# A graph layer on one core: where the normalized rows are kept, how the residual is cut, and when keys and gathered edges are fetched

## The chip, the cores and the metric

One core of one Trainium2 chip. The metric is the device time of one execution in microseconds; the kernel before has a median of 561.38 us in 3 runs (560.37 to 562.74). The names of the engines: TensorE is PE, VectorE is DVE, ScalarE is ACT, GpSimd is POOL, SyncE is SP in the profile.

## The reference

The inputs are 6250 rows x of 96 values, 206250 edges sorted by destination, and a row of 96 values for each edge. What is computed:

```python
h = relu((x - mean(x)) / sqrt(var(x) + 1e-5))       # for each of the 6250 rows
m = h[src] + edge_attr                              # one row of 96 for each of 206250 edges
aggr = segment_sum(m, dst, 6250)
out = x + (1 + eps) * h + relu(aggr @ W1 + b1) @ W2 + b2
```

## The kernel before, in words

**Tiles.** The 6250 nodes make 49 tiles of 128 rows, called blocks where they are destinations. Rows are held with the 128 nodes of a tile on the partitions: `x_sb` and `h_sb` are [128, 49, 96] in float32, `hl` holds h as a high and a low half in float16.

**Two ways to sum over edges.** For 45 blocks (NM = 45) `h[src]` is never gathered. VectorE turns the sources and destinations of a block's edges into one-hot matrices (`chunk`, four chunks to a block, L547), TensorE multiplies them to a count matrix in eight steps (`octet`, L961), ScalarE copies each step to `adj` (L810), and in the following block TensorE multiplies `adj` with `hl` in 49 slots (`sum_slots`, L973). The edges' own rows are summed by 80 matmuls with another one-hot matrix (`sum_edges`, L967); they stand behind octet 2 of each block. For the last 4 blocks (GATHERED = 4, numbered j = 0 to 3) GpSimd gathers: 40 indirect DMAs (L477), each adding 128 rows of h from a copy in HBM (`h_rows`) to edge rows that lie in the buffer `gathered[(j + 1) % 2]`. Their sum, again 80 matmuls (L967 on gathered_edges), is attached to one of the 45 blocks: ATTACHED names it. TensorE waits there for `gather_done`, the landing of all 40, in the middle of its queue.

**Order.** All of it is written out by hand: each engine has one queue of instructions, and semaphores with constants join them. There is no planner.

**Before block 0.** SyncE loads the indices and x; VectorE and GpSimd pack the keys and find where each block's edges start (`e_tab`). Then x is normalized. VectorE takes moments (`moments`, L554) of each tile, turns them to variances (`variance`), ScalarE takes the root (`deviation`), VectorE inverts it (`normal`). This is done in two groups, tiles 0 to 23 and 24 to 48. ScalarE then makes h of the first group, tile by tile (L850), VectorE scales the second (L634) and ScalarE applies the relu at once (L854). `high_part` on ScalarE (L841) and `low_part` on VectorE (L577) make `hl`. ScalarE also checks that the edges are sorted (`falls`, L833); TensorE adds that up at the end of block 0 (L1084), and VectorE reads the sum in block 1 (L665).

**Where h lies.** `h_sb` lies in the edge buffers 1 and 2 of three. So the edges of blocks 1 and 2 go to the two gathered buffers instead (`edge_rows`), and the first gathered loads have to wait for block 1's edge sum, SyncE's load of block 4 for both residuals. `residual` (L660) adds (1 + eps) h to x, in two operations of 24 and 25 tiles, at the end of blocks 1 and 2 on VectorE.

**Loads on SyncE.** Each block's load is four pairs of DMAs (L340 destinations, L341 edge rows). Load b is queued once the edge sum of block b - 3 is done. `load_gathered(0)` stands before load 4, `load_gathered(1)` after load 5, the next two behind the gathered sums that free their buffers. A gathered load is four triples (L348 to L350).

**Keys.** Each pair of blocks needs one window of packed keys (L449, an indirect DMA of GpSimd, 3 buffers). Windows 0 to 2 are fetched ahead of the gathers, each later one between gathers: `FETCH_EVERY = 7` with `FETCH_FIRST = 5`, that is before gathers 5, 12, 19 and so on. A fetch waits until TensorE has turned the keys three windows before it (L956). VectorE reads window q in block 2q - 2 (`pick`, L625).

Of the kernel before, what the change touches and what calls it, by code (L numbers as in the profile page):

```python
# [5 lines left out]
F32 = mybir.dt.float32  # L6
# [16 lines left out]
GT = 10  # L23
TURN = 3
# [10 lines left out]
GATHERED = 4  # L35
ATTACHED = (14, 24, 34, 42)
TAIL_CUTS = (8, 18, 34)
FETCH_EVERY = 7
FETCH_FIRST = 5
STORE_LAG = 7  # L40
SQRT_AFTER = 18
KEYS_AFTER = 20


def build(nc, x, src, dst, edge, w1, b1, w2, b2, eps, out):
# [31 lines left out]
    with ExitStack() as ctx:  # L77
# [6 lines left out]
        def sem(name):  # L84
            return ctx.enter_context(nc.semaphore(name))
# [25 lines left out]

        h_sb = edge_home[:, 1:3, :, :, :].rearrange("p k g t c -> p (k g t c)")[:, 0:NT * C].rearrange("p (t c) -> p t c", c=C)
        packed = adj_home[:, :, :, :].rearrange("p k h n -> p (k h n)").bitcast(I32)[:, 0:2 * DW].rearrange("p (e two) -> p e two", two=2)
# [117 lines left out]
        falls_clear = sem("falls_clear")  # L231
        scaled_ready = sem("scaled_ready")

# [60 lines left out]

        ROWS = [slice(0, HALF), slice(HALF, NT)]

        def all_stored(engine):
# [11 lines left out]
        def edge_rows(b):  # L309
            return gathered[b % 2] if b in (1, 2) else edges[b % TURN]  # L310

# [3 lines left out]
        def _(sp):  # L315
# [118 lines left out]
        def _(pool):  # L434
# [87 lines left out]
        def _(v):  # L522
            link = [0]

            def chain(ins):
                link[0] += 1
                ins.then_inc(link_done, 1)
                v.wait_ge(link_done, link[0])
# [23 lines left out]
            def moments(t0, t1):  # L552
                for t in range(t0, t1):
                    last = nc.vector.bn_stats(bn[:, t, :], x_sb[:, t, :])  # L554
                return last

            def variance(k):
                sl = ROWS[k]
                parts = [bn[:, sl, c:c + 1].rearrange("p t o -> p (t o)") for c in range(6)]
# [8 lines left out]
            def normal(k):  # L568
                v.wait_ge(std_ready, k + 1)
                chain(nc.vector.reciprocal(rstd[:, ROWS[k]], rstd[:, ROWS[k]]))  # L570
                nc.vector.scalar_tensor_tensor(shift[:, ROWS[k]], stat[:, 0, ROWS[k]], -0.5, rstd[:, ROWS[k]],
                                               ALU.mult, ALU.mult).then_inc(norm_ready, 1)
# [43 lines left out]
            nc.vector.tensor_copy(span[:, :], oct_ps[0:1, 0, 0:GCOLS])  # L616
            nc.vector.tensor_copy(ends[:, :], oct_ps[0:1, 0, 512:512 + GCOLS])
# [8 lines left out]

            v.wait_ge(x_in[1], 32)
            chain(moments(HALF, NT))
            pick(0)
            variance(1)  # L630
            normal(1)
            v.wait_ge(norm_ready, 2)
            for t in range(HALF, NT):
                last = nc.vector.tensor_scalar(h_sb[:, t, :], x_sb[:, t, :], rstd[:, t:t + 1], shift[:, t:t + 1], ALU.mult, ALU.add)  # L634
            last.then_inc(scaled_ready, 1)

            def passes_needed():

                v.wait_ge(spread_read, 1)
                nc.vector.tensor_scalar(row[:, :], row[:, :], keep[:, 0:1], None, ALU.mult)  # L640
# [15 lines left out]

            def residual(k):
                v.wait_ge(eps_ready, 1)
                v.wait_ge(hl_ready, k + 1)
                nc.vector.scalar_tensor_tensor(x_sb[:, ROWS[k], :], h_sb[:, ROWS[k], :], eps_sb[:, 0:1], x_sb[:, ROWS[k], :],  # L660
                                               ALU.mult, ALU.add).then_inc(res_ready, 1)
# [31 lines left out]
            def finish(b):  # L693
                v.wait_ge(out_done, b + 1)
                if b >= OBS:
                    v.wait_ge(out_stored[b % OBS], 16 * (b // OBS))
                nc.vector.tensor_tensor(ob[b % OBS][:, :], x_sb[:, b, :], mlp_ps[:, OUT_AT:OUT_AT + C], ALU.add).then_inc(out_ready, 1)  # L697
# [15 lines left out]
            for b in range(NM):  # L713
# [82 lines left out]
        def _(act):  # L796
# [33 lines left out]
            nc.scalar.activation(packed[:, :, 1].bitcast(F32), S_lo, ACT.Copy).then_inc(lows_ready, 1)  # L830
            act.wait_ge(falls_clear, 1)
            act.wait_ge(steps_ready, 1)
            nc.scalar.activation(steps.bitcast(F32), steps, ACT.Relu, scale=-1.0, accum_out=falls[:, 0:1]).then_inc(falls_ready, 1)  # L833

            def deviation(k):
                act.wait_ge(var_ready, k + 1)
                nc.scalar.activation(rstd[:, ROWS[k]], stat[:, 2, ROWS[k]], ACT.Sqrt).then_inc(std_ready, 1)

# [4 lines left out]
            deviation(0)  # L843
            act.wait_ge(norm_ready, 1)
            for t in range(HALF):
                if t == KEYS_AFTER:
                    next_keys(0)
                if t == SQRT_AFTER:
                    deviation(1)
                last = nc.scalar.activation(h_sb[:, t, :], x_sb[:, t, :], ACT.Relu, bias=shift[:, t:t + 1], scale=rstd[:, t:t + 1])  # L850
# [85 lines left out]
        def _(pe):  # L936
# [83 lines left out]
            def next_project(n):  # L1020
# [4 lines left out]
                project(hid, OUT_AT).then_inc(out_done, 1)  # L1025

            for b in range(NM):
                here, behind = attached(b), attached(b - 1)
# [126 lines left out]
```

## Time and profile before

| | us |
|---|---|
| median of 3 runs | 561.38 |
| the profiled execution | 559.85 |
| its span | 558.0 |
| TensorE matmul busy | 499.2 (89%) |
| VectorE busy | 504.6 (90%) |
| ScalarE busy | 375.2 (67%) |
| GpSimd busy | 353.9 (63%) |

The span is what the hardware profiler saw from first to last instruction of this one execution; all times in rows count from its start. Busy shares are means over stages with different limits. In a timeline row the first number is the start, the second the time to the end of the last instruction of the row; square brackets hold the idle time before it and what ended it. Successive matmuls overlap, so a row's time can reach past the start of the next.

### The profile page before, as it was taken

To read this page: it belongs to the slowest core of one execution; us is meant where nothing else is said; L and a number is where in the kernel's file an instruction comes from. 1 tells how busy PE (TensorE), PEld (TensorE's weight loads), DVE (VectorE), ACT (ScalarE), POOL (GpSimd) and SP (SyncE) were. 2 spreads that over 40 slices of the span, in tenths; PEclk is the share of its full clock that TensorE was granted. 3 is DMA by queue.
4 is the path that set the end of the run, shared out by engine and by line. 5 is a ranking of instruction groups with operands and counts; after the bars stand their busy time and mean duration, and the time that the engine had idled before them with its cause. 6 is when DMAs were issued, how large, how long until landed. Compare 5 with 4: busy or idle time off the path is not lost.

```text
span 558.0 us, 23440 instructions
## 1 busy us (share of the span) xinstructions
PE 499.2 (89%) x9695; PEld 474.5 (85%) x9695; DVE 504.6 (90%) x676; ACT 375.2 (67%) x613; POOL 353.9 (63%) x200
## 2 busy tenths in 40 slices
PE   0406798999999999999999999999999999999995
PEld 0305788999999999999999999998998999999994
DVE  7989997999999999899998998998998989999840
ACT  0486556677777757776875677677776776775771
POOL 1400048888888888888888887687686478870000
PEclk9999879999999999999999999999999999999998
DMA  6789849999879888999888889988878687985000
GB/s 196 244 283 286 245 122 318 277 307 271 234 196 234 230 210 207 290 262 236 230 232 215 210 217 266 285 215 224 227 206 223 158 241 179 236 226 172 6 11 18
DMA packets 99109, 120.57 MB, mean 216 GB/s; under 512 B 71160, under 2 KB 72792, under 8 KB 98870
## 3 DMA queue, kind: packets, MB, share of 16 engines
q1 hardware_dynamic: 74854, 108.13, 63.3%
q0 software_dynamic: 24144, 10.89, 15.5%
q8 instruction: 78, 1.28, 0.9%
q14 instruction: 33, 0.27, 0.2%
HBM read 112.50 MB, written 6.48 MB: 213 GB/s over the span
## 4 chain that ended last, share of the span: by engine, by line
PE 76%; SPq 7%; ACT 4%; issue 4%; DVE 3%; DMA 3%; POOL 2%; ACTq 0%; DVEq 0%; POOLq 0%
PE agg_ps L973 27%; PE oct_ps L961 21%; PE agg_ps L967 14%; PE key_ps L986 5%; PE mlp_ps L991 4%; SPq L340 3%; ACT adj L810 3%; POOL gathered_edges L477 2%; PE key_ps L978 2%; PE key_ps L979 2%; SPq L339 1%; SPq L341 1%; DMA win<-packed_keys,row_i 1%; ACT hid L826 1%; DVE lo_hot L547 1%
## 5 line engine op out<-in xcount | busy, mean ns | idle before, releaser
L810 ACT ACTIVATE adj<-oct_ps 128x784 f16<-128x784 f32 x360 | 300.6, 867 | 146.9 <-PE oct_ps L961 141.5
L477 POOL DMA_INDIRECT gathered_edges<-h_rows,gather_src x160 | 317.8, 1986 | 97.6 <-DMA gathered_edges<-in_edge_attr 49.1
L973 PE MATMUL agg_ps<-hl,adj 128*128 128x192 f16 x2205 | 227.7, 247 | 0.9 <-issue 0.8
L547 DVE TENSOR_TENSOR lo_hot<-iota_z,key 128x2048 f16<-128x2048 f16 x180 | 219.4, 1219 | 0.0
L961 PE MATMUL oct_ps<-z,lo_hot 128*128 128x98 f16 x2880 | 191.5, 209 | 25.3 <-DVE lo_hot L547 21.0
L547 DVE TENSOR_TENSOR z<-z_marks,key 128x1568 f16<-128x1568 f16 x180 | 174.6, 970 | 22.1 <-PE oct_ps L961 21.7
L961 PEld LDWEIGHTS oct_ps<-z,lo_hot 128*128 128x128 f16 x2880 | 162.5, 99 | 33.5 <-issue 13.9
L973 PEld LDWEIGHTS agg_ps<-hl,adj 128*128 128x128 f16 x2205 | 177.1, 98 | 1.9 <-issue 1.4
L967 PE MATMUL agg_ps<-edges,hot 128*32 128x96 f32 x3440 | 81.1, 250 | 0.0
L967 PEld LDWEIGHTS agg_ps<-edges,hot 128*32 128x32 f32 x3440 | 71.8, 111 | 6.4 <-issue 0.3
L674 DVE TENSOR_TENSOR hot<-iota_w,rel 128x1280 f32<-128x1280 f32 x49 | 73.1, 1492 | 1.7
L449 POOL DMA_INDIRECT win<-packed_keys,row_i x23 | 30.5, 1326 | 33.2 <-PE key_ps L956 24.2
L986 PE MATMUL key_ps<-aggT,w_sb 96*96 96x128 f32 x180 | 30.2, 290 | 2.0 <-issue 1.7
L826 ACT ACTIVATE hid<-key_ps,b_sb 96x128 f32<-96x128 f32 x90 | 27.1, 354 | 2.2 <-PE mlp_ps L991 1.5
L991 PE MATMUL mlp_ps<-w_sb,hid 97*128 97x96 f32 (+1 forms) x180 | 26.6, 270 | 0.7 <-ACT hid L826 0.7
L986 PEld LDWEIGHTS key_ps<-aggT,w_sb 96*96 96x96 f32 x180 | 20.9, 162 | 7.4 <-issue 1.3
L991 PEld LDWEIGHTS mlp_ps<-w_sb,hid 97*128 97x128 f32 (+1 forms) x180 | 23.6, 191 | 1.7 <-ACT hid L826 0.9
L697 DVE TENSOR_TENSOR ob<-x_sb,mlp_ps 128x96 f32<-128x96 f32 x45 | 11.2, 249 | 15.4 <-PE mlp_ps L991 15.4
L978 PE MATMUL key_ps<-ident,agg 128*96 128x128 f32 x90 | 18.2, 285 | 0.4 <-ACT agg L816 0.4
L979 PE MATMUL key_ps<-ident,agg 128*96 128x128 f32 x90 | 17.4, 276 | 0.0
L816 ACT ACTIVATE agg<-agg_ps 128x192 f32<-128x192 f32 x45 | 14.9, 330 | 3.7 <-PE agg_ps L973 3.2
L798 ACT ACTIVATE key<-key_ps 128x512 f16<-128x512 f32 x23 | 13.8, 600 | 0.4 <-PE key_ps L979 0.4
(126 smaller groups left out, 204.2 us busy)
## 6 DMA issues: line engine op xcount, KB each, us to landing
edges<-in_edge_attr SPq DMA_DIRECT2D x172, 480.0 KB
gathered_edges<-in_edge_attr SPq DMA_DIRECT2D x24, 480.0 KB
dst<-in_dst SPq DMA_DIRECT2D x180, 5.0 KB
gathered_edges<-h_rows,gather_src POOLq DMA_INDIRECT x160
out<-ob SPq DMA_DIRECT2D x45, 48.0 KB
packed_keys<-adj SPq DMA_DIRECT2D x1, 1632.0 KB, 6.3
h_rows<-edges SPq DMA_DIRECT2D x1, 1200.0 KB, 9.2
h_rows<-edges SPq DMA_DIRECT2D x1, 1152.0 KB, 9.2
```

What stands on the lines that cost most here:

```text
L449: nc.gpsimd.indirect_dma_start(out=to[:, :, :].rearrange("p e two -> p (e two)"), out_offset=None, in_=keys_dram, in_offset=bass.IndirectO ...
L477: nc.gpsimd.indirect_dma_start(out=gathered[k][:, g, t, :], out_offset=None, in_=h_dram, in_offset=bass.IndirectOffsetOnAxis(ap=gather_src ...
L547: return nc.vector.tensor_tensor(out.rearrange("p t (w two) -> p t w two", two=2), marks[0:out.shape[0], 0:width].rearrange("p (o w two) - ...
L674: return nc.vector.tensor_tensor(hot[buf][:, :, :], iota_w[:, :].rearrange("p (o w) -> p o w", o=1).broadcast_to([P, GROUPS * GT, GROUP]), ...
L810: return nc.scalar.activation(adj[k][:, :, 2 * OCT * o:2 * OCT * (o + 1)].rearrange("p h (t q) -> p t h q", q=2), oct_ps[:, o % 2, :].rear ...
L826: last = nc.scalar.activation(to[0:C, j, :], key_ps[0:C, at + P * j:at + P * (j + 1)], ACT.Relu, bias=b1_sb[:, j:j + 1])
L961: last = nc.tensor.matmul(oct_ps[:, o % 2, P * t:P * t + ZW], lo_hot[o // 2][:, at, :], z[o // 2][:, at, :], start=True, stop=True)
L967: last = nc.tensor.matmul(sums[GROUP * g:GROUP * (g + 1), :], hots[:, g * GT + t, :], rows[:, g, t, :], start=fresh and t == 0, stop=False ...
L973: last = nc.tensor.matmul(agg_ps[buf][:, 0:2 * C], adj[buf][:, h, :], hl[:, h, :], start=False, stop=(h == NT - 1), skip_group_check=True)
L978: nc.tensor.matmul(key_ps[0:C, TURN_AT:TURN_AT + P], agg[:, 0:C], ident[:, :], start=True, stop=False)
L986: last = nc.tensor.matmul(key_ps[0:C, at + P * j:at + P * (j + 1)], w1_sb[:, j, :], turned_sums[:, :], start=True, stop=True)
L991: last = nc.tensor.matmul(mlp_ps[:, at:at + C], hidden_values[0:C + 1 - j, j, :], w2_sb[0:C + 1 - j, j, :], start=(j == 0), stop=(j == H - 1))
```

## The change

- `h_sb` now lies in the two gathered buffers (tiles 0 to 39 in buffer 0, tiles 40 to 48 in buffer 1). All blocks load their edges into the edge buffers proper, and the third load no longer waits for the order check's input.
- The residual is cut into nine pieces, `RES`: tiles 40 to 48 first, then eight pieces of 5 tiles. They stand at the end of blocks 2 to 10. `finish(b)` waits for the piece that holds its tile.
- The first gathered load (buffer 1) stands behind load 5 and waits for the first piece; the second (buffer 0) stands behind load 14 and waits for all nine.
- ATTACHED goes from (14, 24, 34, 42) to (14, 22, 32, 42).
- The statistics are made in three groups: tiles 0 to 15, 16 to 31, 32 to 48. ScalarE makes h of all 49 tiles, and the order check comes behind the first root.
- The fourth window is fetched at once; later ones at 3 for each 25 gathers, before gathers 0, 9, 17, 25, 34 and so on.

```diff
-ATTACHED = (14, 24, 34, 42)
+ATTACHED = (14, 22, 32, 42)
-FETCH_EVERY = 7
-FETCH_FIRST = 5
+FETCH_EVERY = 25
+FETCH_PER = 3
-SQRT_AFTER = 18
-KEYS_AFTER = 20
+KEYS_AFTER = 24
+RES_FIRST = 40
+RES_ROWS = 5
...
-        h_sb = edge_home[:, 1:3, :, :, :].rearrange(...)
+        h_sb = gather_home[:, :, :, :, :].rearrange(...)
...
+        THIRDS = [slice(0, 16), slice(16, 32), slice(32, NT)]
+        RES = [(RES_FIRST, NT)] + [(t, t + RES_ROWS) for t in range(0, RES_FIRST, RES_ROWS)]
...
-            return gathered[b % 2] if b in (1, 2) else edges[b % TURN]
+            return edges[b % TURN]
... (SyncE)
-            sp.wait_ge(steps_ready, 1)
             load(2)
...
                 sp.wait_ge(edges_done, b - TURN + 1)
-                if b == TURN + 1:
-                    load_gathered(0)
-                    sp.wait_ge(res_ready, 2)
-                    sp.wait_ge(h_stored, 32)
                 load(b)
                 if b == TURN + 2:
+                    sp.wait_ge(h_stored, 32)
+                    sp.wait_ge(res_ready, 1)
+                    load_gathered(0)
+                if b == TURN + 2 + len(RES):
+                    sp.wait_ge(res_ready, len(RES))
                     load_gathered(1)
... (GpSimd)
-            fetched = WINS
+            fetched = WINS + 1
+            fetch(WINS)
             pool.wait_ge(h_stored, 32)
...
-                        if (j * GROUPS + g) * GT + t >= (fetched - WINS) * FETCH_EVERY + FETCH_FIRST and fetched < MPAIRS:
+                        if ((j * GROUPS + g) * GT + t) * FETCH_PER >= (fetched - WINS - 1) * FETCH_EVERY and fetched < MPAIRS:
... (VectorE, before block 0)
-            moments(0, HALF // 2)
+            chain(moments(0, 16))
+            variance(0)
...
+            normal(0)
...
-            chain(moments(HALF // 2, HALF))
-            variance(0)
+            moments(16, HALF)
+            v.wait_ge(x_in[1], 32)
+            moments(HALF, 26)
...
-            normal(0)
+            chain(moments(26, 32))
+            variance(1)
...
-            v.wait_ge(x_in[1], 32)
-            chain(moments(HALF, NT))
             pick(0)
-            variance(1)
             normal(1)
-            v.wait_ge(norm_ready, 2)
-            for t in range(HALF, NT):
-                last = nc.vector.tensor_scalar(h_sb[:, t, :], x_sb[:, t, :], rstd[:, t:t + 1], shift[:, t:t + 1], ALU.mult, ALU.add)
-            last.then_inc(scaled_ready, 1)
+            nc.vector.tensor_copy(span[:, :], oct_ps[0:1, 0, 0:GCOLS])
+            nc.vector.tensor_copy(ends[:, :], oct_ps[0:1, 0, 512:512 + GCOLS]).then_inc(spread_read, 1)
+            chain(moments(32, NT))
+            variance(2)
+            normal(2)
... (VectorE, blocks)
-                if b in (1, 2):
-                    residual(b - 1)
+                if 2 <= b < 2 + len(RES):
+                    residual(b - 2)
... (ScalarE)
+            deviation(0)
             act.wait_ge(falls_clear, 1)
             act.wait_ge(steps_ready, 1)
             nc.scalar.activation(steps.bitcast(F32), steps, ACT.Relu, scale=-1.0, accum_out=falls[:, 0:1]).then_inc(falls_ready, 1)
...
+            for t in range(NT):
+                for k in range(1, 3):
+                    if t == THIRDS[k].start:
+                        deviation(k)
+                for k in range(3):
+                    if t == THIRDS[k].start:
+                        act.wait_ge(norm_ready, k + 1)
+                last = nc.scalar.activation(h_sb[:, t, :], x_sb[:, t, :], ACT.Relu, bias=shift[:, t:t + 1], scale=rstd[:, t:t + 1])
+                if t + 1 == HALF:
+                    last.then_inc(h_ready, 1)
+                if t + 1 == KEYS_AFTER:
+                    next_keys(0)
+                if t + 1 == HALF:
+                    high_part(0)
             last.then_inc(h_ready, 1)
-            high_part(0)
-            act.wait_ge(scaled_ready, 1)
-            nc.scalar.activation(h_sb[:, ROWS[1], :], h_sb[:, ROWS[1], :], ACT.Relu).then_inc(h_ready, 1)
             high_part(1)
```

## Rows read from the trace of the kernel before

**Rows 1.** Page, busy time, share of the span, instructions

```profile
PE 499.2 (89%) x9695; PEld 474.5 (85%) x9695; DVE 504.6 (90%) x676; ACT 375.2 (67%) x613; POOL 353.9 (63%) x200
```

**Rows 2.** Windows: busy us of each engine, granted clock, DMA share, 100 to 500 us

```profile
100.00:500.00 400.00, 395.24 (x7856) 378.66 (x7849) 378.56 (x437) 288.16 (x473) 325.56 (x172) 1.00 0.88 232
```

**Rows 3.** Timeline of TensorE, edge sums: blocks 2, 5, 14, 14 gathered, 22, 34 gathered

```profile
75.92 2.16 PE L967 MATMUL agg_ps<-gathered_edges,hot 128*32 128x96 f32 x80
...
109.77 1.86 PE L967 MATMUL agg_ps<-edges,hot 128*32 128x96 f32 x80
...
204.57 1.86 PE L967 MATMUL agg_ps<-edges,hot 128*32 128x96 f32 x80
206.24 1.83 PE L967 MATMUL agg_ps<-gathered_edges,hot 128*32 128x96 f32 x80
...
292.17 1.86 PE L967 MATMUL agg_ps<-edges,hot 128*32 128x96 f32 x80
...
424.84 1.83 PE L967 MATMUL agg_ps<-gathered_edges,hot 128*32 128x96 f32 x80
```

**Rows 4.** Windows, GpSimd's busy time alone: two rows of L477, then L449

```profile
77.30:177.50 100.20, 78.75 (x40) 1.00 0.92 251
177.50:280.40 102.90, 81.37 (x40) 1.00 0.90 238
...
177.50:280.40 102.90, 7.56 (x6) 1.00 0.90 238
```

**Rows 5.** Waits of the whole kernel: us in total, times, longest

```profile
POOL win L449 <- PE key_ps L956: 24.2, 6, 8.5
```

**Rows 6.** Timeline of GpSimd, first and third gather

```profile
77.37 3.62 POOL L477 DMA_INDIRECT gathered_edges<-h_rows,gather_src  x1 [49.13 <-DMA gathered_edges<-in_edge_attr]
...
83.75 1.68 POOL L477 DMA_INDIRECT gathered_edges<-h_rows,gather_src  x1 [0.30 <-issue]
```

**Rows 7.** Timeline of ScalarE before block 0

```profile
26.29 6.55 ACT L850 ACTIVATE edges<-x_sb,shift,rstd 128x96 f32<-128x96 f32 x18 [1.51 <-DVE shift L571]
...
35.61 2.12 ACT L841 ACTIVATE hl<-edges 128x2304 f16<-128x2304 f32 x1
...
44.35 1.57 ACT L810 ACTIVATE adj<-oct_ps 128x784 f16<-128x784 f32 x2 [0.24 <-PE oct_ps L961]
```

**Rows 8.** Timeline of VectorE, blocks 0 to 4

```profile
39.55 0.20 DVE L668 TENSOR_TENSOR rel<-dst,gbase 128x40 f32<-128x40 int32 x1
...
55.60 0.15 DVE L665 TENSOR_SCALAR keep<-mlp_ps 128x1 f32<-128x1 f32 x1
...
64.30 2.61 DVE L660 SCALAR_TENSOR_TENSOR x_sb<-edges,eps_sb,x_sb 128x2304 f32<-128x2304 f32 x1
66.83 0.19 DVE L668 TENSOR_TENSOR rel<-dst,gbase 128x40 f32<-128x40 int32 x1
...
76.74 2.71 DVE L660 SCALAR_TENSOR_TENSOR x_sb<-edges,eps_sb,x_sb 128x2400 f32<-128x2400 f32 x1
...
95.86 0.29 DVE L625 TENSOR_SCALAR keyT<-win,base 128x128 f32<-128x128 int32 x1 [2.69 <-DMA win<-packed_keys,row_i]
```

**Rows 9.** Timeline of TensorE, end of block 0

```profile
53.08 0.34 PE L1084 MATMUL mlp_ps<-falls,ones 127*128 127x1 f32 x2
```

**Rows 10.** Tile view of the key windows, all 23

```profile
DMA to landing us min/median/max: 4.2/4.9/6.2
```

**Rows 11.** Timeline of SyncE's queue: first gathered load, loads of blocks 4 and 5

```profile
63.81 0.33 SPq L348 DMA_DIRECT2D gather_src<-in_src  x1
...
80.20 0.33 SPq L340 DMA_DIRECT2D dst<-in_dst  x1
...
86.68 0.33 SPq L340 DMA_DIRECT2D dst<-in_dst  x1
```

**Rows 12.** Windows, columns as in rows 2, TensorE in block 2

```profile
70.60:76.00 5.40, 5.38 (x46) 5.00 (x50) 5.40 (x7) 2.57 (x3) 0.00 (x0) 0.50 0.71 193
```

More of the change, by code:

```diff
@@ L110, in build @@
         keyT = [sb(f"keyT{k}", [P, P]) for k in range(2)]
-        h_sb = edge_home[:, 1:3, :, :, :].rearrange("p k g t c -> p (k g t c)")[:, 0:NT * C].rearrange("p (t c) -> p t c", c=C)
+        h_sb = gather_home[:, :, :, :, :].rearrange("p k g t c -> p (k g t c)")[:, 0:NT * C].rearrange("p (t c) -> p t c", c=C)
         packed = adj_home[:, :, :, :].rearrange("p k h n -> p (k h n)").bitcast(I32)[:, 0:2 * DW].rearrange("p (e two) -> p e two", two=2)
@@ L231, in build @@
         falls_clear = sem("falls_clear")
-        scaled_ready = sem("scaled_ready")
         win_in = [sem(f"win_in{k}") for k in range(WINS)]
@@ L557, in variance @@
             def variance(k):
-                sl = ROWS[k]
+                sl = THIRDS[k]
                 parts = [bn[:, sl, c:c + 1].rearrange("p t o -> p (t o)") for c in range(6)]
@@ L569, in normal @@
                 v.wait_ge(std_ready, k + 1)
-                chain(nc.vector.reciprocal(rstd[:, ROWS[k]], rstd[:, ROWS[k]]))
-                nc.vector.scalar_tensor_tensor(shift[:, ROWS[k]], stat[:, 0, ROWS[k]], -0.5, rstd[:, ROWS[k]],
+                chain(nc.vector.reciprocal(rstd[:, THIRDS[k]], rstd[:, THIRDS[k]]))
+                nc.vector.scalar_tensor_tensor(shift[:, THIRDS[k]], stat[:, 0, THIRDS[k]], -0.5, rstd[:, THIRDS[k]],
                                                ALU.mult, ALU.mult).then_inc(norm_ready, 1)
@@ L615, in _ @@
             nc.vector.tensor_scalar(e_tab[:, :], e_raw[:, :], float(ELAST), None, ALU.min).then_inc(tab_ready, 1)
-            nc.vector.tensor_copy(span[:, :], oct_ps[0:1, 0, 0:GCOLS])
-            nc.vector.tensor_copy(ends[:, :], oct_ps[0:1, 0, 512:512 + GCOLS])
             nc.vector.tensor_copy(reach_row[:, :], key_ps[0:1, 2 * P:3 * P]).then_inc(spread_read, 1)
-            normal(0)
+            chain(moments(26, 32))
+            variance(1)
             def pick(q):
@@ L625, in pick @@
                 nc.vector.tensor_scalar(keyT[q % 2][:, :], win[q % WINS][:, :, 0], base[:, q:q + 1], 1.0 / SPREAD, ALU.subtract, ALU.mult).then_inc(keys_ready, 1)
-            v.wait_ge(x_in[1], 32)
-            chain(moments(HALF, NT))
             pick(0)
-            variance(1)
             normal(1)
-            v.wait_ge(norm_ready, 2)
-            for t in range(HALF, NT):
-                last = nc.vector.tensor_scalar(h_sb[:, t, :], x_sb[:, t, :], rstd[:, t:t + 1], shift[:, t:t + 1], ALU.mult, ALU.add)
-            last.then_inc(scaled_ready, 1)
+            nc.vector.tensor_copy(span[:, :], oct_ps[0:1, 0, 0:GCOLS])
[3 more added lines that the diff above has]
+            normal(2)
             def passes_needed():
-                v.wait_ge(spread_read, 1)
+                v.wait_ge(spread_read, 2)
                 nc.vector.tensor_scalar(row[:, :], row[:, :], keep[:, 0:1], None, ALU.mult)
@@ L655, in passes_needed, with residual @@
                 nc.vector.tensor_scalar(need_i[:, 3:4], need[:, 0:1], float(MAXR), None, ALU.min).then_inc(need_ready, 1)
[L657 to L660, printed above, removed]
+            def residual(piece):
+                rows = slice(*RES[piece])
+                if piece == 0:
+                    v.wait_ge(eps_ready, 1)
+                    v.wait_ge(hl_ready, 2)
+                nc.vector.scalar_tensor_tensor(x_sb[:, rows, :], h_sb[:, rows, :], eps_sb[:, 0:1], x_sb[:, rows, :],
                                                ALU.mult, ALU.add).then_inc(res_ready, 1)
@@ L694, in finish @@
                 v.wait_ge(out_done, b + 1)
+                if b < RES_FIRST:
+                    v.wait_ge(res_ready, 2 + b // RES_ROWS)
                 if b >= OBS:
@@ L830, in _ @@
             nc.scalar.activation(packed[:, :, 1].bitcast(F32), S_lo, ACT.Copy).then_inc(lows_ready, 1)
-            act.wait_ge(falls_clear, 1)
-            act.wait_ge(steps_ready, 1)
-            nc.scalar.activation(steps.bitcast(F32), steps, ACT.Relu, scale=-1.0, accum_out=falls[:, 0:1]).then_inc(falls_ready, 1)
             def deviation(k):
                 act.wait_ge(var_ready, k + 1)
-                nc.scalar.activation(rstd[:, ROWS[k]], stat[:, 2, ROWS[k]], ACT.Sqrt).then_inc(std_ready, 1)
+                nc.scalar.activation(rstd[:, THIRDS[k]], stat[:, 2, THIRDS[k]], ACT.Sqrt).then_inc(std_ready, 1)
             def high_part(k):
@@ L843, in _ @@
             deviation(0)
-            act.wait_ge(norm_ready, 1)
-            for t in range(HALF):
-                if t == KEYS_AFTER:
+            act.wait_ge(falls_clear, 1)
+            act.wait_ge(steps_ready, 1)
+            nc.scalar.activation(steps.bitcast(F32), steps, ACT.Relu, scale=-1.0, accum_out=falls[:, 0:1]).then_inc(falls_ready, 1)
+            for t in range(NT):
[9 more added lines that the diff above has]
+                if t + 1 == KEYS_AFTER:
                     next_keys(0)
-                if t == SQRT_AFTER:
-                    deviation(1)
-                last = nc.scalar.activation(h_sb[:, t, :], x_sb[:, t, :], ACT.Relu, bias=shift[:, t:t + 1], scale=rstd[:, t:t + 1])
+                if t + 1 == HALF:
+                    high_part(0)
             last.then_inc(h_ready, 1)
-            high_part(0)
-            act.wait_ge(scaled_ready, 1)
-            nc.scalar.activation(h_sb[:, ROWS[1], :], h_sb[:, ROWS[1], :], ACT.Relu).then_inc(h_ready, 1)
             high_part(1)
@@ L1025, in next_project @@
                 project(hid, OUT_AT).then_inc(out_done, 1)
+            pe.wait_ge(spread_read, 2)
             for b in range(NM):
```

## The prediction

> **What bounds the kernel now.** I read the page's busy lines first: TensorE is busy 89% of the span and GpSimd only 63% [rows 1], so GpSimd looks idle enough to be ignored. It can't be, as the next views show. Between 100 and 500 us TensorE is busy 395.24 of 400 us at full clock [rows 2]: in the steady part it is the bound and has nothing to catch up with, so whatever stops it there is lost. TensorE's timeline gives the places: the first gathered sum starts at 206.24 (block 14), block 22's own edge sum at 292.17, the third gathered sum at 424.84 (block 34) [rows 3]. The row of block 22 matters most: a gathered sum attached to block 22 would start 1.67 us after that edge sum (206.24 less 204.57), at 293.84. The windows over GpSimd's gathers show that the first 40 gathers take 100.2 us and the second 40 take 102.9 us [rows 4]. Of the 102.9, the busy time is 81.37 + 7.56, the rest is 0.30 between instructions, so GpSimd works through without a pause; it waits only 24.2 us in all, before window fetches [rows 5], and those are late ones (its longest is 8.5 us). The four times 40 gathers are one serial chain of some 400 us, which starts with the first gather at 77.37 [rows 6]. The second 40 end at 280.4 and are used in block 24, two pitches after block 22, near 315: 35 us of slack. That slack is what the change spends.
>
> **Part 1, three groups, ScalarE makes all of h.** VectorE loses 25 scalings at the start; ScalarE does 49 tiles instead of 24, at 6.55 / 18 = 0.36 us each [rows 7]. VectorE must still finish the third group's statistics before block 0, and their root stands behind ScalarE's tile 31. ScalarE: check of the order done near 22.9, 16 tiles to 28.8, then a wait for the second group until about 30.4 (its factors stand behind the first key window on VectorE), 8 tiles to 33.3, key copy 0.6, high part 2.12 [rows 7] to 36.0, 8 tiles to 38.9, root, and VectorE's last factors at 39.6. Block 0 started at 39.55 [rows 8]. So nothing is gained there: estimate 0, between -1 and +1.
> ScalarE then makes 17 more tiles (6.2) and the second high part (2.2) and comes to block 0's sums at 48.1 instead of 44.35 [rows 7]. That is 3.8 us late. VectorE hides most of it, since it has buffers for a block ahead, until it reads the order check's result in block 1: that product ran at 53.08, behind block 0's last octet, and moves to about 57.6, while VectorE would read it at 55.60 [rows 8, 9]. Cost up to 2.3 us, with 0 as the other end.
>
> **Part 2, the residual.** Blocks 1 and 2 lose operations of 2.61 and 2.71 us, about 5.2 together (64.30 to 66.83 is 2.53) [rows 8]. These stood on VectorE, which has no idle time until 95.86. The nine pieces: 2.53 us for 2304 elements is about 1.04 ns each plus some 0.1; 480 elements take 0.6, the first of 864 takes 1.0. Blocks 2 and 3 get 1.6 back; blocks 4 to 10 have seven of 0.6, against TensorE's pitch: nine blocks from 109.77 to 204.57 [rows 3], 10.53 each. VectorE is busy 378.56 of 400 us [rows 2], 10.0 of each 10.53, so with a piece its block takes 10.6: cost 0 to 0.7.
>
> **Part 3, the fetches.** The fourth window is fetched at once. In block 4 VectorE waited 2.69 us for it, from 93.2 to 95.86 [rows 8]; this goes. Later windows come every 8.33 gathers, about 20.9 us for two blocks of 21, and each window is asked for more than a block before it is needed: the fifth, sent with the first gather near 97, lands after 4.2 to 6.2 us [rows 10], and block 6 wants it near 113. No cost.
>
> The start therefore gains, by block 5: 5.2 - 1.6 + 2.7 - 2.3 = 4.0, less about 0.5 for what TensorE still needs by itself: 3.5. After the pieces 2.9 is left. If the gathers were in time, that would be the result.
>
> **Part 4, where the gathers start.** The buffers now hold h, so the first gathered loads are queued one block later and behind one more load. Before, they were issued from 63.81, and the first gather came at 77.37, 13.56 later [rows 6, 11]. Now SyncE first waits for block 2's edge sum, which ended at 75.92 + 2.16 = 78.08 [rows 3]. In the changed kernel VectorE starts block 2 between 2.5 us earlier and 0.2 earlier (2.53 gained, 2.3 lost): I take 76.6. Then 0.7 to the first issue, 6.48 for a block's load (80.20 to 86.68) [rows 11], and 12 to 13.56 for the gathered loads and their landing. First gather: 76.6 + 0.7 + 6.5 + 12.8 = 96.6, range 93.5 to 99. That is 19 us later than 77.37.
>
> **Part 5, the chain to block 22.** With 8.33 gathers per fetch each of the first two blocks has 5 fetches. The first: 100.2 as before. The second: 102.9 less one fetch of 1.5 (7.56 / 6, and 0.3 between) is 101.4 [rows 4]. Three corrections. The first gather took 3.62 where the following ones take 1.7 [rows 6]: it lay beside the large residual operation, which now is elsewhere (-1.7). The small pieces lie beside gathers: 0 to 0.6 each for six of them; I take +1.5. When TensorE stops, VectorE soon stops too and the gathers run faster: the shortest takes 1.54 + 0.30 against 2.33 on average, for some 6 us: -1.2. Sum: 201.6 - 1.4 = 200.2, between 197 and 205. Landing of the last gather after GpSimd's issue is not shown; windows land 4.2 to 6.2 after their start [rows 10], so 3.0 to 5.0 after the issue of 1.2; I take 3.5. Ready: 96.6 + 200.2 + 3.5 = 300.3.
> The first of these three corrections is where a rule and a row differ. The first gather (77.37 to 80.99) ends exactly 1.54 after the residual operation's end at 79.45, as though it had been held back all the while [rows 6, 8]. The Trainium skill (SBUF — State Buffer, Who interferes with whom) says that a VectorE instruction with two SBUF inputs holds up only GpSimd's reads, and infers that it does not hold up descriptor generation. By that rule the pieces would cost the gathers nothing and the chain would be 1.5 us shorter; the single row speaks against it.
>
> **Part 6, what it costs.** Block 22 wants the rows at 293.84 - 2.9 = 290.9. TensorE stands for 9.4 us. Against the kernel before, where it would go on at 293.84 with nothing to wait for, the net shift is 300.3 - 293.8 = +6.5: the gain at the start cancels out of this, since TensorE waits for GpSimd whatever it arrives at. And the clock: after VectorE kept TensorE idle before 70.6 its granted clock was 0.50 of full (1.2 GHz) from 70.6 to 76.0, 5.38 us busy [rows 12]; the same work at 2.4 GHz is 2.7 us. I add 2.7, between 0 and 3.5.
> The Trainium skill (TensorE: Matmul & The Clock Gate, What's actually happening) has the same two levels and says that an idle TensorE falls to the lower; it agrees with this row.
> After block 22 nothing stalls again. Gathers three end near 297 + 100 + 3.5 = 400.5, and block 32 comes at about 300.3 + 2.7 + 109 = 412 (20 blocks with two attached ones took 218.6, from 206.24 to 424.84 [rows 3]); gathers four near 499, block 42 near 521. At block 14: ready at 96.6 + 98.5 to 101.7 + 3.5, at most 201.8, wanted at 203.3. A late arrival there would only use up time that block 22 loses anyway. The second gathered load is issued after block 11's edge sum and lands near 193, before the 195 at which it is wanted; the margin is thin.
> Sum: 6.5 + 2.7 = +9.2. The profiled execution took 559.85 for a span of 558.0; it lies 1.5 below the median of 561.38, so the forecast is span 567.2, median 561.38 + 9.2 = 570.6.
>
> **The rivals.**
> 1. The gathers are in time and the start's gain stays. For it: page and waits call GpSimd idle a third of the time. Against it: that idle time is the 49.1 us before the first gather and the end. It needs readiness by 290.9, 9.4 us earlier, so first gather by 87.2 or 2.1 us per gather for 2.33. Time: 561.4 - 2.9 = 558.5; faster. Chance 0.08.
> 2. The stall exists but is small: first gather at 93.5, chain 197, landing 3.0, no clock loss: ready at 293.5, shift -0.3 to about +2.5. Time 561 to 564, no change. Chance 0.08.
> 3. The stall is larger, or a second one comes: the second gathered load is late (SyncE reaches it behind stores), or windows come too late because their fetches now ride on gathers that start 19 us later. Each gather block's wait adds 3 to 8 us: 574 to 579, slower. For it: the load's thin margin. Against it: the windows' lead of more than a block. Chance 0.14.
> 4. ScalarE's late start delays block 0 further and half clock holds TensorE through blocks 1 to 3: 2 to 3 us, but every microsecond passes one for one to the first gather. Time 572 to 574, slower; it is inside the main case's range. Chance 0.10.
> The forecast itself has 0.60. Half a per cent, 2.8 us, is about what a measurement can tell from no change: faster 0.08, same 0.08, slower 0.84. The range takes the main case from 565 to 575 and reaches into rivals 2 and 3: 563.5 to 577.
>
> **What would show it.** The first gather of the changed kernel between 93.5 and 99. A wait of TensorE of about 9 us in block 22, ahead of the gathered edge sum, ended by a gather's landing, and the only long one; clock at 0.5 behind it. No VectorE wait in block 4, edge sum of block 5 about 3.5 earlier than at 109.77. GpSimd without waits for keys. Wrong it would be if gathers went at clearly under 2.3 us each, or if the first began before 90; then rival 1 decides.

## The result, and the profile after

The changed kernel takes 565.30 us (median of 10 runs, 562.94 to 567.96), the one before 559.13 in ten runs beside it (557.05 to 562.74; the 561.38 of the forecast was the median of the first three of them). The ratio is 1.010, with 95% between 1.0072 and 1.0129: slower by 6.2 us. Runs more than 1.5% above the fastest of the same kernel are left out of every ratio here, so a ratio need not be the quotient of the two medians. Forecast was slower by 9.2, to 570.6. The mechanism was right; the size forecast was half as large again as the one measured.

The profiled execution took 564.01 us for a span of 562.1, so the two traces lie only 4.1 us apart. The busy line of its page, and a row of its waits (us in total, times, longest):

```profile
PE 499.5 (89%) x9695; PEld 473.1 (84%) x9695; DVE 500.5 (89%) x666; ACT 382.0 (68%) x638; POOL 347.3 (62%) x200
```

```profile
PE agg_ps L977 <- issue: 6.3, 3, 5.4
```

Busy times are what they were [rows 1]; nothing in the totals shows a loss. GpSimd's wait before its chain has grown from 49.1 us [rows 6] to 62.3, its waits for keys [rows 5] are gone but for half a microsecond, and TensorE has two new waits, both ahead of gathered sums. TensorE's timeline shows where (L977 is the old L967): blocks 2, 14, 14 gathered, 22, 22 gathered.

```profile
70.79 1.86 PE L977 MATMUL agg_ps<-edges,hot 128*32 128x96 f32 x80
...
199.03 1.86 PE L977 MATMUL agg_ps<-edges,hot 128*32 128x96 f32 x80
201.93 1.86 PE L977 MATMUL agg_ps<-gathered_edges,hot 128*32 128x96 f32 x80 [1.04 <-DMA gathered_edges<-h_rows,gather_src]
...
290.57 1.86 PE L977 MATMUL agg_ps<-edges,hot 128*32 128x96 f32 x80
297.86 3.72 PE L977 MATMUL agg_ps<-gathered_edges,hot 128*32 128x96 f32 x80 [5.43 <-issue]
```

Read against [rows 3]: block 2 is 5.1 us early, block 14 still 5.5, block 22 only 1.6, since block 14 lost 1.0 to the gathers and 2.25 in a gap behind. The gap belongs to this execution: in a second trace of the same kernel (experiment 2) it is missing, block 22 comes 2.2 us sooner, and the wait there is 8.10 us. Block 22's gathered sum could have started at 292.24 and starts at 297.86. "issue" in the bracket means that this view finds no releaser. I take it to be the landing of the gathers, which TensorE's program waits for at this place; GpSimd's timeline holds the first and the last of them:

```profile
92.67 3.25 POOL L451 DMA_INDIRECT win<-packed_keys,row_i  x1 [62.31 <-DMA gathered_edges<-in_edge_attr]
96.22 2.61 POOL L480 DMA_INDIRECT gathered_edges<-h_rows,gather_src  x1 [0.30 <-issue]
...
292.61 2.22 POOL L480 DMA_INDIRECT gathered_edges<-h_rows,gather_src  x1 [0.30 <-issue]
```

The second 40 gathers are issued by 294.83, and TensorE goes on 3.03 us after. TensorE's granted clock behind that wait is 0.50, in a window of 5.2 us:

```profile
297.80:303.00 5.20, 5.14 (x87) 4.78 (x88) 0.00 (x0) 0.00 (x0) 4.29 (x4) 0.50 1.03 279
```

GpSimd's gathers (busy time alone), the first and the second 40:

```profile
92.60:197.10 104.50, 82.30 (x40) 1.00 0.89 236
197.30:294.90 97.60, 76.58 (x40) 1.00 0.91 241
```

### The profile page after: what moved, and what is told of

Its sections match the earlier page's. It is cut to its first block, busy times and chain, and to the rows that moved or that the text cites. A ratio compares the mean times of both kernels' runs of the same rounds, so it can differ in the third digit from the quotient of the medians.

```text
span 562.1 us, 23456 instructions
## 1 busy us (share of the span) xinstructions
PE 499.5 (89%) x9695; PEld 473.1 (84%) x9695; DVE 500.5 (89%) x666; ACT 382.0 (68%) x638; POOL 347.3 (62%) x200
## 4 chain that ended last, share of the span: by engine, by line
PE 57%; POOL 16%; SPq 8%; issue 7%; ACT 4%; DVE 4%; DMA 3%; ACTq 0%; DVEq 0%; POOLq 0%
PE agg_ps L983 20%; PE oct_ps L971 15%; POOL gathered_edges L480 14%; PE agg_ps L977 12%; PE key_ps L996 4%; SPq L342 3%; PE mlp_ps L1001 3%; ACT adj L817 2%; SPq L341 2%; POOL win L451 2%; SPq L343 2%; PE key_ps L988 1%; PE key_ps L989 1%; DMA gathered_edges<-h_rows,gather_src 1%; DVE lo_hot L550 1%
## 5 line engine op out<-in xcount | busy, mean ns | idle before, releaser
L480 POOL DMA_INDIRECT gathered_edges<-h_rows,gather_src x160 | 310.0, 1937 | 48.8 <-issue 48.8
L971 PEld LDWEIGHTS oct_ps<-z,lo_hot 128*128 128x128 f16 x2880 | 160.8, 99 | 32.4 <-issue 18.3
L977 PE MATMUL agg_ps<-edges,hot 128*32 128x96 f32 x3600 | 85.5, 249 | 0.9 <-issue 0.9
L977 PEld LDWEIGHTS agg_ps<-edges,hot 128*32 128x32 f32 x3600 | 75.3, 111 | 7.1 <-issue 0.7
L451 POOL DMA_INDIRECT win<-packed_keys,row_i x23 | 31.7, 1377 | 74.0 <-DMA gathered_edges<-in_edge_attr 62.3
L857 ACT ACTIVATE gathered_edges<-x_sb,shift,rstd 128x96 f32<-128x96 f32 x49 | 17.9, 453 | 1.1 <-DVE shift L574 1.1
```

The source lines that it names most:

```text
L451: nc.gpsimd.indirect_dma_start(out=to[:, :, :].rearrange("p e two -> p (e two)"), out_offset=None, in_=keys_dram, in_offset=bass.IndirectO ...
L480: nc.gpsimd.indirect_dma_start(out=gathered[k][:, g, t, :], out_offset=None, in_=h_dram, in_offset=bass.IndirectOffsetOnAxis(ap=gather_src ...
L971: last = nc.tensor.matmul(oct_ps[:, o % 2, P * t:P * t + ZW], lo_hot[o // 2][:, at, :], z[o // 2][:, at, :], start=True, stop=True)
L977: last = nc.tensor.matmul(sums[GROUP * g:GROUP * (g + 1), :], hots[:, g * GT + t, :], rows[:, g, t, :], start=fresh and t == 0, stop=False ...
```

## The experiments

All runs but four (named below) were made on chips where the kernel before takes 559 to 561 us. Each ratio is against the kernel before on the same chip.

**1. The attachment list alone.** Three kernels; first the changed one with the old list:

```diff
-ATTACHED = (14, 22, 32, 42)
+ATTACHED = (14, 24, 34, 42)
```

> The changed kernel with the old attachment list (14, 24, 34, 42). Theory (the gathers start 15 us later and TensorE waits for them in blocks 14 and 22): the wait in block 22 and the half clock behind it go; the gathered sum of block 14 still starts about 1 us late. The trace of the changed kernel was 1.6 us ahead of the one before at block 22's own edge sum, so this ends 1 to 2 us under the kernel before, about 557.5. Rival A (the nine residual pieces, the three groups or the new pace of the fetches cost the time themselves, all along): the list changes nothing, 564 to 566.

Measured: 556.41 us, ratio 0.9927 (0.9898 to 0.9956). The loss is gone and a gain is there; only block 14 still waits (1.7 us in this trace). Next, a first block two later:

```diff
-ATTACHED = (14, 22, 32, 42)
+ATTACHED = (16, 24, 34, 42)
```

> The changed kernel with the attachment list (16, 24, 34, 42). Theory: no gathered sum is waited for any more; the lead of 5.5 us that the changed kernel had at block 13 is kept to the end: 559.1 - 5.5 = 553.6, between 553 and 555.5. Rival A: 564 to 566. Rival B (only block 22 matters, block 14's loss was a stall of instruction supply that has nothing to do with the gathers): as the list (14, 24, 34, 42), about 557.5.

Measured: 554.24 us, ratio 0.9893 (0.9858 to 0.9927), and twice more, once on another chip, 555.19 (0.9912, 0.9878 to 0.9947) and 555.27 (0.9916, 0.9894 to 0.9939). The expectations of those two:

> The changed kernel with the list (16, 24, 34, 42), again. Theory: 1% faster than the kernel before on either kind of chip, since nothing in it waits for a gather; 10 to 11 us under the changed kernel where there are no gaps in the supply, 0 to 4 where there are.

> Nine pieces with the list (16, 24, 34, 42), the third time. Expected 0.9 to 1.1% under the kernel before, as twice before.

This kernel beats both: the one before by 4 to 7 us in its three runs, the changed one by 10.5 on the chip that ran both. All of the change is in it but the list. How much of that is block 14's is less clear. Theory had 2 to 4 us for it, and the three medians lie 1.1 to 2.2 us under the 556.41 of the list (14, 24, 34, 42); rival B (nothing) is unlikely but not excluded. And the new list in the kernel before:

```diff
-ATTACHED = (14, 24, 34, 42)
+ATTACHED = (14, 22, 32, 42)
```

> The kernel before with the new attachment list (14, 22, 32, 42) alone. Theory: the second 40 gathers are done at 280.4 plus a landing of 3, and block 22 wants them at 293.8, so nothing waits: the kernel before within 1 us. Rival C (attaching to block 22 and 32 costs by itself, by the order of the work around it): 4 to 6 us over the kernel before.

Measured: 559.08 us, ratio 0.9975 (0.9947 to 1.0003). Its trace has no wait at block 22. So the list costs nothing by itself, the rest of the change costs nothing by itself, and the two together lose 1%. Rival A (pieces, groups and fetches cost the time themselves) and rival C (the early attachment costs by itself) are out.

**2. The start of the chain, moved both ways.** The first gathered load ahead of load 5:

```diff
-                load(b)
                 if b == TURN + 2:
                     sp.wait_ge(h_stored, 32)
                     sp.wait_ge(res_ready, 1)
                     load_gathered(0)
+                load(b)
```

> The changed kernel with the first gathered load queued ahead of load 5, not behind it. Theory: the whole chain of gathers starts 6.5 to 7 us earlier (first window fetch near 86 for 92.7), the second 40 are ready near 291.2 for 297.9; block 14 no longer waits; block 22 waits about 3 us, perhaps without the half clock. Time: 291.2 - 293.8 = -2.6 against the kernel before, plus 0 to 2.7 for the clock: 556.5 to 559.5. Rival A: no change against the changed kernel, 564 to 566.

Measured: 561.05 us, ratio 0.9957 (0.992 to 0.9994); its single runs spread from 554.4 to 565.3. The median is level with the 560.77 of the kernel before on this chip, 4 us under the changed kernel, and over the 556.5 to 559.5 expected. The gathered sum of block 22 starts at 293.86, 4.0 us earlier than in the changed kernel. The mechanism held, the distance did not: the chain starts at 89.5 instead of 86, since the load now waits for the first residual piece (the piece ends at 75.43, the load is issued at 76.57). Then one block later (`TURN + 3` for `TURN + 2`):

> The changed kernel with the first gathered load one block later, again, now beside the changed kernel on one chip. Theory: ready 10 us later, so 9 to 11 us over the changed kernel where its blocks wait for gathers; on a chip with gaps the part that the slower TensorE leaves, 3 to 8. Rival A: within 2 us.

and the changed kernel again, beside it on one chip:

> The changed kernel itself, beside the ones below on one chip, since the last call ran on a chip where TensorE stood for instructions in many small gaps (0.2 to 0.4 us each) and everything took 14 to 18 us longer. Where TensorE is slower and the gathers keep their pace, the gathers come in time: on such a chip theory expects the changed kernel 0 to 1% faster than the one before; on one without the gaps 0.7 to 1.3% slower, as first measured. Rival A (the cost is in pieces and fetches): slower by the same share on both.

Measured: the later one 568.88 us (1.0144, 1.0082 to 1.0206), the changed one 565.67 (1.0088, 1.0053 to 1.0123). Slower by 3.2, where 9 to 11 was expected: a miss. The later kernel's single runs spread from 563.6 to 574.9, so the 3.2 is known to a few us only, but not as 9. TensorE's timeline of the later one in block 22, then GpSimd's windows:

```profile
294.94 1.86 PE L977 MATMUL agg_ps<-edges,hot 128*32 128x96 f32 x80
301.90 2.41 PE L977 MATMUL agg_ps<-gathered_edges,hot 128*32 128x96 f32 x55 [5.11 <-issue]
```

```profile
104.10:201.80 97.70, 75.81 (x40) 1.00 0.93 244
201.80:299.20 97.40, 76.27 (x41) 0.98 0.87 230
```

The chain starts 10.4 us after the changed kernel's that was run beside it (93.8) and its rows are taken 3.5 us later (301.90 for 298.36): the first 40 took 97.7 instead of 103.9 (93.8 to 197.7). One gather more falls into the second window's edges. The difference in time, 3.2, fits the 3.5 by which the rows are late. What does not hold is that the chain keeps its length. The 6.2 us are found in single gathers: in the changed kernel's trace three of the first 40 take 3.9 us, some 2 us over the others, and in the later kernel's none does. Experiment 3 takes these up.

**3. What sets the length.** Two residual pieces, neither beside a gather:

```diff
-RES_ROWS = 5
+RES_ROWS = 40
```

> The changed kernel with two residual pieces, again, beside the changed kernel. On the chip with gaps its first 40 gathers with 5 fetches took 100.6 us against 104.4 in the changed kernel's trace. Theory P: the second 40 are ready 3 to 4 us earlier than in the changed kernel, and where block 22 waits for them the time is 2 to 4 us less although VectorE spends 3.6 us more in block 3. Theory Q: the two are equal within 1.5 us.

Measured, beside the changed kernel: 563.93 us (1.0054, 1.0018 to 1.0089) for 565.67. Rows of TensorE and GpSimd's windows:

```profile
290.11 1.86 PE L977 MATMUL agg_ps<-edges,hot 128*32 128x96 f32 x80
294.55 2.02 PE L977 MATMUL agg_ps<-gathered_edges,hot 128*32 128x96 f32 x80 [2.58 <-issue]
```

```profile
93.10:191.90 98.80, 77.19 (x40) 0.99 0.91 246
191.90:288.80 96.90, 75.64 (x41) 1.00 0.91 236
```

98.8 for 103.9: in these two traces the rows are ready 3.8 us earlier. The medians differ by 1.7, between the 2 to 4 of theory P and the 1.5 of theory Q, with VectorE having 3.5 more to do in block 3. The trace of the two pieces is that of the fastest of its twelve runs (558.50), so it shows more than the median does. Whether the pieces are what costs the gathers 5 us, the next kernel asked. In the changed kernel three gathers take 3.9 us (at 113.83, 135.04 and 156.27), each across a piece with the comparison behind it. The first of them, and VectorE's comparison:

```profile
113.83 3.90 POOL L480 DMA_INDIRECT gathered_edges<-h_rows,gather_src  x1 [0.30 <-issue]
```

```profile
117.08 1.49 DVE L679 TENSOR_TENSOR hot<-iota_w,rel 128x1280 f32<-128x1280 f32 x1
```

The kernel with the pieces in the middle of their blocks:

```diff
-                for c in range(2, CHUNKS):
-                    chunk(b, c)
                 if 2 <= b < 2 + len(RES):
                     residual(b - 2)
+                for c in range(2, CHUNKS):
+                    chunk(b, c)
```

> The changed kernel (list 14, 22, 32, 42) with each residual piece between chunks 1 and 2 of its block instead of behind chunk 3, where relative and comparison follow. Theory P2 (a gather is held while float32 operations of VectorE with two SBUF inputs follow each other for over 2 us: piece, relative, comparison): no gather of 3.9 us is left in blocks 5 to 10, the first 40 gathers with 5 fetches take 98 to 100.5 us for 104, the second 40 are ready 4 to 6 us earlier; the time is 3 to 6 us under the changed kernel (0.9 to 1.0% over the kernel before), so within 0.5% of the kernel before. Theory Q (the long gathers come from elsewhere, as the queue of transfers): chain 104, time 0.9 to 1.0% over the kernel before.

Measured: 563.05 us, ratio 1.0066 (1.0048 to 1.0084). In between: the chain's first part is 101.8, the rows are taken at 294.16, and two long gathers are there after all, the first of them here:

```profile
103.20 4.65 POOL L480 DMA_INDIRECT gathered_edges<-h_rows,gather_src  x1 [0.30 <-issue]
```

No piece runs between 102.3 and 112.2 in that kernel, only the comparison at 106.46. Theory P2 as I stated it falls. The traces go further: a piece is neither needed nor enough for a long gather. Not needed, since the kernel before with the new list (experiment 1), whose residual is long done by then, has four of them in its first 40, here the first and the comparison that it runs across:

```profile
120.05 4.02 POOL L477 DMA_INDIRECT gathered_edges<-h_rows,gather_src  x1 [0.30 <-issue]
```

```profile
122.68 1.49 DVE L674 TENSOR_TENSOR hot<-iota_w,rel 128x1280 f32<-128x1280 f32 x1
```

Its first 40 take 108.6 us (75.35 to 183.96), where the kernel before, which is the same program up to block 22, took 100. Not enough, since in experiment 2 the later start has six pieces beside its first 40 gathers, not one gather over 2.9 us, and 97.7 us. In all 17 traces 44 gathers take 3.8 us or more; a piece lies beside 27 of them and none beside 17. All 44 start 2.6 to 3.3 us before a comparison and run into it, but many that start there are not long. On the usual chips the first 40 take 98 to 100 us in the traces with none or one of them, 102 with two, 102 to 105 with three. So 98.8 against 103.9 is one long gather against three. With nine pieces at the end of their blocks, nine of ten traces have three or four in the first 40, with two pieces it is one or two in four traces; the pieces may well favour them, but that they cause them is not shown. What makes a gather long stays open.

**4. Nine pieces or two, with nothing waiting for gathers** (list 16, 24, 34, 42):

> Two pieces with the list (16, 24, 34, 42), beside the next run on one chip. VectorE spends 4.2 us in block 3 for 0.6, nine pieces give 1.3 back by block 13. Expected 2 to 3 us over the next run. Rival: equal.

Measured: 559.25 us (0.9972, 0.9947 to 0.9997) beside 555.27 for nine pieces. 4.0 us, over the 2 to 3 expected: nine pieces over nine blocks are the better form, 0.71 us each where VectorE had 0.5 idle, against one of 4.21 in block 3.

**5. Four runs on a slower chip.** There the kernel before took 578.96 us:

> The changed kernel with the first gathered load one block later (behind load 6). Theory (the time is set by when the second 40 gathers are ready, one for one): the chain starts about 10.5 us later, block 14 waits about 10 us more than in the changed kernel, block 22 is reached later by that and the second 40 are ready near 308; the time is 10 to 11 us over the changed kernel, about 575. Rival A (slack is left in the chain, the cost is elsewhere): within 2 us of the changed kernel, 564 to 567.

> The changed kernel with the residual in two pieces, tiles 40 to 48 at the end of block 2 and tiles 0 to 39 at the end of block 3, so that none lies beside a gather; the second gathered load then stands behind load 7. Theory P (a residual piece holds GpSimd's gathers up for as long as it runs): the first 40 gathers with their 5 fetches take about 100 us for 104.4, the second 40 are ready near 293.4 for 297.9. Theory Q (VectorE's operations with two inputs do not hold up the making of descriptors): 104.4 as before. VectorE is the bound in block 3, so 3.6 us of the lead go there; time with P 559 to 562, with Q 563.5 to 566.

> As the run with two pieces, with the attachment list (16, 24, 34, 42), so that no gathered sum is waited for. It measures what nine pieces over nine blocks are worth by themselves against 4.2 us of VectorE in block 3: lead at block 5 about 3.2 for 6.8 us, of which the nine pieces give 1.3 back up to block 13. Expected 2 to 2.5 us over the kernel with nine pieces and this list: 556 to 557. Rival: pieces are hidden in either place: 554 to 554.5.

> The changed kernel with the list (16, 24, 34, 42) and without the early fetch of the fourth window: it is fetched with the first gather. Block 4 wants it at 88.6 and it would land at 92.7 + 5 = 97.7; VectorE waits 9 us there, TensorE 7. Expected 7 us over the kernel with this list, 561 to 562: then the early fetch does not gain the 2.7 us that VectorE waited before, it avoids a wait of 9 which the later start of the gathers would have made. Rival: the wait is hidden by buffers, 556 to 557.

The last one:

```diff
-            fetched = WINS + 1
-            fetch(WINS)
+            fetched = WINS
```

Neither the changed kernel nor the one with nine pieces and the list from 16 was run on this chip, and the kernel before has no trace there, so of the expectations only those on the traces can be held against the runs directly. Measured: one block later 576.18 (0.9963, 0.993 to 0.9996), two pieces 574.47 (0.9937, 0.9905 to 0.9968), two pieces with the list from 16 574.26 (0.9932, 0.9904 to 0.9961), no early fetch 583.86 (1.009, 1.0057 to 1.0124). The first is a miss: about 575 was expected for a usual chip, 10 us over the changed kernel and so 16 over the kernel before; here it is not slower than the kernel before. The waits are there: its trace (of its slowest execution, 585.64) has 5.56 us in block 14 and 5.38 in block 22, which TensorE reaches at 303.7. Why it is no slower than the kernel before all the same is not shown. Its first 40 gathers take 104.1 us with three long ones, against the 97.7 and none of the same kernel in experiment 2. The two pieces have no wait in block 22, and their first 40 take 100.6 us, near the 100 of theory P, with two long ones among them; as nothing waits, the list from 16 changes nothing either (574.26 for 574.47). The fetch is clear in its size if not to the microsecond, 9.6 us over the kernel next to it, which has two pieces for nine, with VectorE's wait in block 4:

```profile
99.39 0.29 DVE L629 TENSOR_SCALAR keyT<-win,base 128x128 f32<-128x128 int32 x1 [9.38 <-DMA win<-packed_keys,row_i]
```

9.38 us, where 9 were expected. The early fetch is not a gain of the 2.69 us of [rows 8] put on top; it pays for the later start of GpSimd's chain. In the same trace GpSimd waits 5.55 us before gather 41 for the second gathered load: the wait that rival 3 feared.

## Why the prediction was right in kind and too large

**Right.** The slack of 35 us in the second 40 gathers was spent by a start 15.3 us later (77.37 to 92.67) and an attachment two blocks, some 21 us, earlier. The long wait stands in block 22 (5.4 and 8.1 us in two traces of the changed kernel, about 9 forecast), it goes away with the old list, the clock behind it is 0.50, and the start's gain cancels: readiness decides. In six traces on the usual chips that wait there, span less the start of block 22's gathered sum is 264.2, 266.7, 264.2, 264.8, 262.0 and 266.1; in the kernel before, 558.0 - 293.84 = 264.2, where 2.5 us of gaps happen to stand for the 2.7 us of the clock. The clock term was sized right: from that sum (297.86) to block 23's edge sum at 311.16 pass 13.30 us, behind block 14 of the kernel before 10.58 (206.24 to 216.82); 2.7 forecast, 2.7 found. VectorE's wait in block 4 is gone.

**The terms that were off.** Ready at 300.3 was forecast, 297.86 came.

- Part 4, the start: "I take 76.6" for block 2's edge sum; it ended at 70.79 + 1.86 = 72.65. This is the step that failed. It has three parts. Block 0 starts on VectorE at 37.66, not 39.6 (part 1 had said that nothing is gained there, within 1 us): the second group's factors did not wait for the key window until 30.4 but were there at 28.8, as the window was there at 27.86. The order check cost VectorE 1.13 us, not 2.3. And I took the distance of 11.25 us from VectorE's block start to the edge sum's end over from a trace in which TensorE stood at half clock there [rows 12]; here TensorE is at full clock from 66 to 73 and the distance is 9.03 (63.62 to 72.65). The first gathered load was issued at 80.67, 3.1 us before the 83.8 of the forecast, and 12.0 us passed from there to the start of the chain instead of 12.8: -3.9 together. The sign named for this, the first gather between 93.5 and 99, came true at 96.22 by luck: a window fetch stands ahead of that gather, and the chain, whose start is what the sum puts at 96.6, began at 92.67. For the same reasons block 5's edge sum came 6.8 us early for 3.5 forecast, which changes nothing behind block 22.
- Part 5, the length: 200.2 forecast, 202.2 found (92.67 to 294.83). The sum hid two larger errors: the first part took 104.4 instead of 100.0 (three gathers of 3.9), the second 97.8 instead of 100.2. That the first part can be 97.7, 98.8 or 108.6 by the number of its long gathers is something that the sum had no term for, and that the two errors partly cancel is luck. I had the pieces at +1.5. By the inference in the Trainium skill (SBUF — State Buffer, Who interferes with whom) they would cost nothing; experiment 3 leaves open whether they do. The single row that I set against it, the first gather's end 1.54 us behind the residual's, is no special case: nearly all gathers end so behind a change of instruction on VectorE (last section).
- Landing: 3.5 forecast, 3.03 found.
- Block 14 was forecast with 1.5 us to spare and came 1.0 late; as forecast, this has no price of its own, since block 22 waits anyway.

Readiness by itself makes 4.0 of the 6.5 forecast, with the clock 6.7, against 6.2 measured in ten runs. The two traces show 4.1, because TensorE in the kernel before has gaps of 0.57, 0.82 and 1.11 us in blocks 22, 30 and 34 that the other trace has not.

**The base.** 561.38 was 2.2 us high; a forecast of a difference should have been read so.

**A sentence that was wrong although the result did not show it.** Rival 4 said that every microsecond passes one for one to the first gather, and its time took it from there to the end. In the one pair of traces that tries it, 10.4 us at the start of the chain became 3.5 at its end; the rest went into long gathers that one has and the other has not. And rival 1 needs 2.2 us per gather, not 2.1: its 9.4 us are 0.12 for each of 80.

## What to carry to other kernels

An engine that the profile's page calls 62% busy can be the one that sets the time, if its work is one chain with a fixed first and last point: compute the chain's end and the consumer's arrival, and treat their difference as a budget that every edit of start and consumer draws on. Two edits that are harmless alone can overdraw it together. When a constant is tuned (here the list), retune it after the edits that move its inputs: (16, 24, 34, 42) turned a loss of 1% into a gain of 1%. And leave room in the budget: the length of the same 40 gathers differed by 6 to 9 us between two traces of the same instructions (97.7 and 104.1, 100 and 108.6).

## What the runs showed of the hardware that was not expected

**Chips differ by 18 us in the same program.** On the slower one, TensorE has many gaps with no releaser inside a row of 80 matmuls. The same kernel (two pieces) on it, TensorE's timeline in a block, and its window beside that of the usual chip:

```profile
242.53 1.14 PE L977 MATMUL agg_ps<-edges,hot 128*32 128x96 f32 x29
244.03 1.35 PE L977 MATMUL agg_ps<-edges,hot 128*32 128x96 f32 x51 [0.36 <-issue]
```

```profile
100.00:500.00 400.00, 389.03 (x7541) 367.41 (x7540) 363.11 (x420) 276.84 (x455) 332.24 (x179) 1.00 0.86 224
```

```profile
100.00:500.00 400.00, 394.36 (x7801) 377.36 (x7802) 376.40 (x435) 289.11 (x473) 331.29 (x177) 1.00 0.88 231
```

The first window is the slower chip's: 7541 matmuls in 400 us for 7801, at full clock, while GpSimd does as much on both (179 and 177 instructions). With TensorE slower and the gathers not, the two pieces no longer wait in block 22, where they wait 2.58 us on the usual chip. What makes the gaps is not shown; that they sit in the supply of instructions is my reading of "issue".

**Gathers go at the pace of VectorE.** In steady blocks gathers follow each other every 2.0 us or a little more (83.75, 85.74, 87.75 in the kernel before), which is the time of one chunk on VectorE (2.02). In block 22 of the changed kernel, where VectorE stands for 9.3 us, they come every 1.85 (296.98, 298.83, 300.68). The tie is closer than that: in the changed kernel's trace 73 of the first 80 gathers end within 0.06 us of the moment 1.54 us after an instruction of VectorE started, and 66 to 75 of 80 do in the other traces; 1.54 us is what a gather takes while VectorE stands. So a gather seems to be held until VectorE changes from one instruction to the next, and then runs beside it. It does not explain why the first 40 of experiment 2 were shorter, since nothing waits there. That VectorE sets the pace is read from these rows, not tried by itself.
